# Attention and feed-forward block in float16 pairs on one core: start, weight norms and the order of four steps are rearranged

## The reference

```
x: 4096 tokens (4 sequences of 1024) x 512
x = x + layernorm(attn(layernorm(x)))     # qkv = x @ w_qkv.T + b; 16 heads of 32;
                                          # chunks of 128 tokens, decaying state carried between chunks
                                          # out = attn @ w_out.T + b_out
x = x + layernorm(ffn(layernorm(x)))      # gate, up: 512 -> 1536, down: 1536 -> 512
                                          # weights of ffn rounded to float8 e4m3, scaled by column
gate = silu((x @ e4m3(gate_w)) * gate_scale);  up = (x @ e4m3(up_w)) * up_scale
y = ((gate * up) @ e4m3(down_w)) * down_scale
```

## Time and profile before

| what | us |
|---|---|
| median of 3 runs (1008.97 to 1009.78) | 1009.73 |
| the profiled execution, its own time | 1009.62 |
| its span | 1007.8 |
| TensorE busy | 950.2 (94%) |
| VectorE busy | 666.4 (66%) |
| ScalarE busy | 526.3 (52%) |
| GpSimd busy | 685.0 (68%) |

### The profile page before, as it was taken

How to read it: one execution, slowest core, us unless ns; L and a number is a source line. 1 busy time by engine, 2 the same in 40 slices (tenths; PEclk the granted TensorE clock), 3 DMA queues, 4 the chain that set the end, 5 groups by cost and what they waited for, 6 DMA issues and landing times.

```text
span 1007.8 us, 21799 instructions
## 1 busy us (share of the span) xinstructions
PE 950.2 (94%) x8396; PEld 703.3 (70%) x8396; DVE 666.4 (66%) x1342; ACT 526.3 (52%) x997; POOL 685.0 (68%) x837
## 2 busy tenths in 40 slices
PE   1999997999887999999999999999999999999996
PEld 1777775767665778677786767878677786776764
DVE  7977776765787766676776657766666676766422
ACT  3656565476553646354564545546354564544522
POOL 2788988787756768576685857758567685756633
PEclk9999998999999999999999999999999999999999
DMA  9699799999939957749396693947759386621110
GB/s 345 188 247 257 194 258 251 305 229 253 270 93 217 207 126 154 132 117 196 65 175 119 134 162 90 189 97 146 135 125 190 77 167 118 124 63 43 33 33 21
DMA packets 297640, 159.86 MB, mean 159 GB/s; under 512 B 141632, under 2 KB 272832, under 8 KB 297408
## 3 DMA queue, kind: packets, MB, share of 16 engines
q1 hardware_dynamic: 296672, 157.86, 69.9%
q10 hardware_dynamic: 864, 0.61, 0.2%
HBM read 82.93 MB, written 41.94 MB: 124 GB/s over the span
## 4 chain that ended last, share of the span: by engine, by line
PE 49%; POOL 26%; DVE 12%; issue 5%; ACT 3%; DMA 3%; SPq 1%; POOLq 0%; DVEq 0%; ACTq 0%
PE bank L858 17%; PE bank L844 14%; PE att L821 8%; POOL att_pool L998 6%; POOL w_pool L1012 4%; POOL hl L1008 3%; POOL rstd L939 3%; PE bank L737 3%; PE bank L752 3%; POOL xr L1004 2%; DVE stats L1243 2%; DMA dram_qk<-qk_hl 2%; POOL rstd L943 2%; POOL vv L982 2%; PE att L737 2%
## 5 line engine op out<-in xcount | busy, mean ns | idle before, releaser
L844 PE MATMUL bank<-f_pool,gate_q 128*128 128x256 f16 x1536 | 184.8, 274 | 5.3 <-DMA f_pool<-hl 4.3
L844 PE MATMUL bank<-f_pool,up_q 128*128 128x256 f16 x1536 | 183.7, 273 | 0.0
L858 PE MATMUL bank<-down_q,w_pool 128*128 128x512 f16 x768 | 168.3, 379 | 8.1 <-POOL w_pool L1012 8.1
L998 POOL TENSOR_TENSOR att_pool<-p,att_pool 128x512 f16<-128x512 f32 x128 | 145.6, 1158 | 37.6 <-ACT att_pool L527 37.6
L1374 DVE SCALAR_TENSOR_TENSOR w_pool<-bank,us_t,w_pool 128x256 f32<-128x256 f32 x192 | 84.1, 479 | 126.1 <-PE bank L844 100.7
L844 PEld LDWEIGHTS bank<-f_pool,gate_q 128*128 128x128 f16 x1536 | 147.8, 98 | 25.9 <-DMA f_pool<-hl 4.5
L844 PEld LDWEIGHTS bank<-f_pool,up_q 128*128 128x128 f16 x1536 | 150.6, 98 | 17.6
L936 POOL TENSOR_TENSOR rstd<-mv,eps_t 128x1 f32<-128x1 f32 (+1 forms) x112 | 28.9, 258 | 172.6 <-DVE mv L1246 172.6
L858 PEld LDWEIGHTS bank<-down_q,w_pool 128*128 128x128 f16 x768 | 74.1, 98 | 96.4 <-issue 9.5
L1012 POOL TENSOR_TENSOR w_pool<-w_pool 128x512 f16<-128x512 f32 x96 | 111.0, 1158 | 42.4 <-ACT w_pool L579 42.4
L527 ACT CAST att_pool<-p 128x512 f16<-128x512 f32 x128 | 76.7, 619 | 65.8 <-DVE p L1284 65.8
(11 more groups left out here) (141 smaller groups left out, 1789.2 us busy)
## 6 DMA issues: line engine op xcount, KB each, us to landing
xr<-in_x SPq DMA_DIRECT2D x32, 512.0 KB, 4.6
dram_qk<-qk_hl SPq DMA_DIRECT2D x64, 256.0 KB, 5.4
att_pool<-dram_qk SPq DMA_DIRECT2D x64, 256.0 KB, 6.4
f_pool<-dram_qk SPq DMA_DIRECT2D x64, 256.0 KB, 6.4
dram_v<-vv SPq DMA_DIRECT2D x32, 256.0 KB, 3.8
dram_kd<-kd_hl SPq DMA_DIRECT2D x32, 256.0 KB, 3.3
qn_pool<-dram_qk SPq DMA_DIRECT2D x32, 256.0 KB, 7.8
out_x<-w_pool SPq DMA_DIRECT2D x32, 256.0 KB, 2.1
```

What stands on the lines that cost most here:

```text
L844: ins = nc.tensor.matmul(b[:, j * TOK:(j + 1) * TOK], w[:, k, o * P:(o + 1) * P], x1_hl[:, v % 2, part, k], start=(k == 0 and part == 0), ...
L858: ins = nc.tensor.matmul((b_gate, b_up)[t][:, :], h_hl[:, part, k, t * P:(t + 1) * P], down_q[:, k], start=(k == 0 and part == 0), stop=(k ...
L998: nc.gpsimd.tensor_tensor(pr_hl[:, 1, heads(g)], by_head(p32[:, g % 2]), pr_hl[:, 0, heads(g)], ALU.subtract).then_inc(p_lo_d, 1)
```

## The change

The weights are loaded by columns (q, k, v) and each third gets its own scale; x of unit 0 comes in two halves; v's weights are issued behind turn_x(0); down_s moves from ScalarE's queue to SP's. third() is now all four row tiles by 256 columns. TensorE runs 48 products of constants before the first spread and 16 behind it. The squares and their sums are gone: VectorE takes the row maximum of each rounded piece (row_limit), squares and sums twelve numbers a partition (row_sums), and one product sums them over the partitions (sum_rows, in ahead(12)); scale_h moves behind the lead. kd_hi(k) and kd_lo(k) move into ahead(k). In early(1) the steps of x1 move forward on VectorE, ScalarE and GpSimd. down runs in four parts: products 0 to 9 of both token tiles, then 10 and 11 of both, with later waits.

```diff
         def third(w, part, half):
-            return w[:, 2 * half:2 * half + 2, part * D:(part + 1) * D]
+            return w[:, :, part * D + half * TOK:part * D + (half + 1) * TOK]
...
-            load_x(0)
-            for k in range(KT):
-                sp.dma_start(w_stage[:, k], w_qkv_t[k * P:(k + 1) * P, :]).then_inc(w_in[k], 16)
+            for t in range(T):
+                sp.dma_start(xr[:, 0, t], x_u[0][:, t]).then_inc(x0_in[t], 16)
+            for part in range(3):
+                if part == 2:
+                    turn_x(0)
+                sp.dma_start(w_stage[:, :, part * D:(part + 1) * D],
+                             w_qkv_t.rearrange("(k p) n -> p k n", p=P)[:, :, part * D:(part + 1) * D]
+                             ).then_inc(w_in[part], 16)
             load_x(1)
-            turn_x(0)
@@ ScalarE @@
+            w_hi(0)
+            w_hi(1)
             x_normalise(1)
             x_hi(1)
+            w_hi(2)
 
             def ahead(k):
                 if k:
                     v_hi(k - 1)
                 q_hi(k, 0)
-                if k:
-                    kd_hi(k - 1)
                 q_hi(k, 1)
-                if 2 <= k < 14:
-                    square(k - 2)
                 k_hi(k, 2)
...
                     x_hi(k + 2)
+                kd_hi(k)
@@ TensorE @@
+            def sum_rows():
+                pe.wait_ge(eps_d, 3)
+                pe.wait_ge(row_sum_d, 1)
+                nc.tensor.matmul(b_gate[:, 0:4], ones, row_sum[:, :], start=True, stop=True).then_inc(row_sum_mm, 1)
...
             def ahead(k):
                 if k == 2:
                     spread_wout_max()
                 project_qk(k, 0)
+                if k == 0:
+                    spread_w_max(1)
                 project_qk(k, 1)
+                if k == 0:
+                    spread_w_max(2)
                 project_qk(k, 2)
                 project_qk(k, 3)
-                for n in SUMMED.get(k, ()):
-                    sum_squares(n)
+                if k == 12:
+                    sum_rows()
...
-                down(v, 0)
-                down(v, 1)
+                if projects:
+                    for first, last in ((0, IT - 2), (IT - 2, IT)):
+                        for t in range(T):
+                            down(v, t, first, last)
+                else:
+                    for t in range(T):
+                        down(v, t, 0, IT)
...
+            pe.wait_ge(eps_d, 3)
+            for n in range(48):
+                nc.tensor.matmul(b_up[:, 0:2 * P], warm[:, 0:P], warm, start=True, stop=True)
+            spread_w_max(0)
+            for n in range(16):
+                nc.tensor.matmul(b_up[:, 0:2 * P], warm[:, 0:P], warm, start=True, stop=True)
...
-            def down(v, t):
-                if t == 0:
-                    pe.wait_ge(silu_d, 6 * v + 6)
-                    pe.wait_ge(h_lo_d, 6 * v + 5)
-                for k in range(IT):
-                    if t == 0 and k == IT - 2:
+            def down(v, t, first, last):
+                for k in range(first, last):
+                    if t == 0 and k == 0:
+                        pe.wait_ge(silu_d, 6 * v + 6)
+                        pe.wait_ge(h_lo_d, 6 * v + 4)
+                    elif t == 0 and k == IT - 4:
+                        pe.wait_ge(h_lo_d, 6 * v + 5)
+                    elif t == 0 and k == IT - 2:
                         pe.wait_ge(h_hi_d, 6 * v + 6)
                         pe.wait_ge(h_lo_d, 6 * v + 6)
+                    elif t and k == 0:
+                        pe.wait_ge(h_d, 6 * v + 6)
@@ GpSimd, ahead(k) @@
-                if k:
-                    kd_lo(k - 1)
                 q_lo(k, 1)
                 if k + 2 < units:
                     x_lo(k + 2)
+                kd_lo(k)
@@ VectorE, prepare_qkv @@
+                w_limit(0, 0)
+                w_limit(0, 1)
+                w_scale(0)
+                scale_bias(0)
+                w_limit(1, 0)
+                w_lo(0, 0)
+                w_lo(0, 1)
+                w_limit(1, 1)
+                w_limit(2, 0)
+                w_scale(1)
+                w_limit(2, 1)
+                scale_bias(1)
+                w_lo(1, 0)
+                x_moments(1, 0)
+                w_lo(1, 1)
+                x_moments(1, 1)
+                w_scale(2)
+                scale_bias(2)
+                w_lo(2, 0)
+                w_lo(2, 1)
...
+            def row_limit(n):
+                dve.wait_ge(f_q_d, n + 1)
+                ins = nc.vector.tensor_reduce(row_max[:, n:n + 1], piece_out(n), AX.X, ALU.max,
+                                              apply_absolute_value=True)
+                ins.then_inc(row_max_d, 1)
@@ VectorE, ahead(k) @@
                 k_lo(k, 3)
+                if k < 12:
+                    row_limit(k)
                 if k == 12:
-                    scale_h()
+                    norms()
...
-            norms(2)
-            flag_down()
+            scale_h()
```

More of the change, by code:

```diff
@@ L131, in sandwich @@
         b_y = [att[:, 0:D], att[:, D:2 * D]]
-        w_in = [sem(f"w_in{k}") for k in range(KT)]
+        w_in = [sem(f"w_in{part}") for part in range(3)]
+        x0_in = [sem(f"x0_in{t}") for t in range(T)]
         eye_in = sem("eye_in")
@@ L461, in _, with w_hi @@
         def _(act):
-            def w_hi(dst, src):
-                nc.scalar.activation(dst, src, ACT.Copy, scale=small[:, 11:12]).then_inc(w_hi_d, 1)
-            def square(n):
-                act.wait_ge(f_q_d, n + 1)
-                at_least(act, square_mm, n - 1)
-                nc.scalar.activation(squares(n), piece_out(n), ACT.Square, scale=SQUARE).then_inc(square_d, 1)
+            def w_hi(part):
+                act.wait_ge(w_scale_d, part + 1)
+                for half in range(2):
+                    nc.scalar.activation(third(wqkv_hi, part, half), third(w_stage, part, half), ACT.Copy,
+                                         scale=small[:, 60 + part:61 + part]).then_inc(w_hi_d, 1)
             def normalised(ln, dst, src, t):
@@ L586, in _ @@
             act.dma_start(us_t[:, :], up_s).then_inc(scl_in, 16)
-            act.dma_start(ds_t[:, :], down_s).then_inc(scl_in, 16)
-            x_normalise(0)
-            x_hi(0)
-            act.wait_ge(w_scale_d, 1)
-            for part in range(3):
-                for half in range(2):
-                    w_hi(third(wqkv_hi, part, half), third(w_stage, part, half))
+            for t in range(T):
+                act.wait_ge(rs_d[LN_X], t + 1)
+                normalised(LN_X, x_src(0)[:, t], x_src(0)[:, t], t).then_inc(nrm_d[LN_X], 1)
+                act.wait_ge(nrm_d[LN_X], t + 1)
+                nc.scalar.copy(x_half(0)[:, t, 0], x_src(0)[:, t]).then_inc(x_hi_d, 1)
+            w_hi(0)
+            w_hi(1)
             x_normalise(1)
             x_hi(1)
+            w_hi(2)
             def ahead(k):
@@ L1173, in w_lo @@
+            def w_lo(part, half):
+                dve.wait_ge(w_hi_d, 2 * part + half + 1)
+                nc.vector.scalar_tensor_tensor(out=third(wqkv_lo, part, half), in0=third(w_stage, part, half),
+                                               scalar=col(60 + part), in1=third(wqkv_hi, part, half), op0=ALU.mult,
                                                op1=ALU.subtract).then_inc(w_lo_d, 1)
```

183 lines of the change are left out of this document (91 added, 92 removed).

## The result

The changed kernel takes 1001.0 us (median of 5 runs, 998.17 to 1003.27) where the kernel before took 1009.73: a ratio of 0.9914, 95% interval 0.9893 to 0.9935. Measured again beside the first experiments it took 1002.28 (1000.12 to 1004.48, 6 runs; ratio 0.9924, 0.9909 to 0.9938). It is faster by some 8 us. The forecast of 993.4 promised 16.3; 1001.0 lies in its range, but the gain is little more than half of the forecast's, and it came by another road than any case in the forecast. The profiled execution took 999.63 with a span of 997.8.

The account below looks back on a forecast made before the run. Bound taken as TensorE, so only its idle time or products removed could count. Terms 3.4 - 15.6 + 0.4 - 2.7 - 1.8 = -16.3 took 1009.7 to 993.4 us; range 983 to 1005.

Parts of the forecast that it names:

- rival B: Start keeps its lead (-4) and slots get no new wait (-7 instead of -1.8): 982 to 987 us; chance 0.18.
- the start, +3.4: Start up to unit 2: first projection sooner, but v(0) and unit 2 later, unit 2 at 59.9 instead of 56.46: +3.4 us.
- the lead, -15.6: Units 2 to 13: sums of squares, TensorE's waits for squares and slow products go, 204.9 to 189.3 us: -15.6.
- rival C: Units 7 to 13 bound by transfers, gain shrinks by 8 to 1001 us, with a worse start 1007; chance 0.19.
- the opened ring: In the units, VectorE-GpSimd-VectorE cycle of 16.7 us through kd_lo of the unit before, claimed to open as kd_lo moves.
- rival D: Units 2 to 11: ring lengthened by the reduction to 18.4 us a unit, total 1020 us, slower than before; chance 0.08.
- step 3: First two units with attention: scale_h and ds_t ahead of masked(0,0,0) +0.4 us; x1 sooner in early(1) -2.7 us.
- x1 sooner, -2.7: Early(1): x1's transposes go out at 320.3 instead of 322.9, gate_up(0,0) starts near 324.6 instead of 327.32: -2.7 us.
- the slots, -1.8: Slots, down in four parts: 8.1 us of waits at down go, a new wait for product(v+1,0) costs 6.3: -1.8 us.

Follow-up runs that it names:

- v's weights first: Changed kernel with w_hi(2) put ahead of x_normalise(1) and x_hi(1) on ScalarE: 999.02 us, ratio 0.9892.
- kd's spill sooner: Changed kernel with SP spilling kd(k) right after the turn of unit k+2, ahead of the loads, instead of one unit later: 993.66 us, ratio 0.9856.
- x1 late: Changed kernel with x1's steps of early(1) put back behind the second attention pass on VectorE, ScalarE and GpSimd: 1001.95 us, ratio 0.9925.
- the second trace: Profiled run of the changed kernel, unchanged, measured again beside the first group of experiments: 1002.28 us, ratio 0.9924.
- kd back in all units: Changed kernel with kd's casts of unit k-1 put back inside unit k on ScalarE and GpSimd, in all units: 1027.16 us, ratio 1.0179.
- kd of unit 13 late: Changed kernel with only kd_hi(13) and kd_lo(13) put back into early(0), behind the first probabilities: 998.29 us, ratio 0.9886.
- the nine traces of the table: Traces of the changed kernel twice and seven variants that don't touch this stretch, in which the cast of kd(13) waits for the spill; no single time.

## Why the prediction was right and wrong

Its direction and its range came true, and so did the mechanisms of the start, the lead and the slots. The total did not come by the sum: early(0), which it had at +0.4, took 5.7 more, and this is nearly all that the gain fell short. Two small sums in the text are off and decide nothing. Ten times 0.4 and three times 0.85 are 6.6, not 6.3. And rival B takes 4 for the step from -1.8 to -7, which is 5.2, so its lower end is 981 and not 982; the stated range, from 983, doesn't reach it either way.

**Right in sum, by some luck: the start, +3.4.** It measured +3.04, with v(0) at 35.64 (forecast 35.9), unit 1 at 43.17 (41.1 to 42.4) and unit 2 at 59.50 (59.9). Two errors cancelled. The first projection came at 15.6 rather than 17.4, because the bias landed earlier, and of no use, since v(0) waits for ScalarE; and limits' large reduction ended at 57.4, so that the spread at 58.83 did not wait for it as forecast, while the v products behind the pause lost 2.35 us (7.69 instead of 5.34) instead of 1. That an earlier v(0) is worth something, and that ScalarE's order sets it, is shown by v's weights first.

**Right: the lead, -15.6.** It measured -16.86. The row maximum takes 1.736 us on f16 data, forecast 1.75 from the f32 reduction of this width (1.748): 16-bit data gain nothing. That agrees with the Trainium skill, "VectorE: DVE Perf Modes", "The perf-mode tier table", by which a reduction has only the 1x form. The 1 us for transfers and the 0.4 for spreads weren't needed, and rival C (transfers bound) did not come about on TensorE: the share rose to 1.11 and units kept 15.66. The reason given, the opened ring, is shown by putting it back: 18.35 us a unit for the 18.4 of rival D. The reduction also slows GpSimd by nothing, as the prediction had it: at 63.05 to 64.79 it runs beside kd_lo, which takes its usual 2.27.

**Wrong: step 3, "+0.4" for early(0).** The step priced scale_h and ds_t (2.4 and 1.15); they took 2.0 together and kept nothing waiting long. What it left out is that kd_hi(13), moved into unit 13, has a wait of its own, for the spill of kd(12), and that v_hi, probs_hi and q_hi of early(0) are queued behind it on ScalarE and state_decay behind kd_lo(13) on GpSimd. The text even wrote "kd_lo(13) is gone from GpSimd there" as a gain. The earlier trace rows could not show the wait, since kd_hi stood so late before that its buffer was always free. But ScalarE's waits held its like: the casts of v waited 10.6 us for spills of v, the last time ahead of v(13). From there the wait could be found by asking of the moved instruction what must have ended before it, and following SP's queue, where the spill stood behind loads of unit 1 and the spill of v(12). Measured: +6.1, of which kd's spill sooner takes away all but 0.45.

The closest rival, C, spoke of spills that grow late in the units but put its price on TensorE's projection, not on what follows the lead. Its number, 1001, matches the median by accident.

**Mis-sized: x1 sooner, -2.7.** The gate came some 2 us sooner, and the next wait, for silu, took nearly all of it back. Over early(1) and the head together the term measured -1.2 in the first trace and +0.5 in the second, and the totals with x1 late and sooner (1001.95; 1001.0 and 1002.28) show no difference. The step had stopped at the gate.

**Right in mechanism, with two sizes that cancel: the slots, -1.8.** It measured -1.08. The old wait, forecast and listed at 8.1, was worth 10.4. The new one, forecast at 6.3 and listed at 5.9 in 13 waits, cost 8.2, and the parts' order 1.1 on top of it, 9.3 together. Both terms came out larger than forecast, by 2.3 and 3.0, so the sum came out nearly right. The forecast saw the new wait but kept to the sum of the change as it stood.

## What to carry to other kernels

When a step is moved earlier, look up what it overwrites, who still reads that, and where the reader's transfer stands in its queue: a wait that never showed becomes a link in the chain, and its price falls where the slack of the stage ends, here at the first instruction after the lead. A wait that a profile lists off the critical path (65 us on ScalarE) deserves a look at the stage's last turn. And where a change has a cure for a wait in two layers (later waits, and parts), measure each alone: one of them may hold the whole gain and the other give it back.

## What the runs showed of the hardware

- A listed pause of TensorE costs more than itself. In the slots 0.35 us listed cost 0.51 from row to row, and taking away 8.1 listed made the slots 10.4 shorter. Behind a pause of 4.48 us, 24 products took 5.30 us instead of 2.78, half the pace for nearly all of them (4.48 us in the second trace, behind 5.34); behind one of 5.91 us, 24 wider ones took 7.69 instead of 5.34, half the pace for somewhat under half of them.
- The same pause of 2.33 us ahead of the same 24 products was followed by 2.78 us in one run and by 4.1 to 4.5 in four. The first products' pace could not be told from the pause alone.
- The transfer of v's bias, 256 KB, let VectorE start on the biases at 5.61 us or before in one trace (kd back in all units) and at 9.87 in another (kd of unit 13 late).
- A spill of two times 256 KB at the end of the lead let its buffer go 6.7 us after it was issued, where the median of this transfer from issue to landing is 3.6 us over the whole kernel. In the nine traces of the table the cast behind it started 4.1 to 9.1 us after unit 13's end.
- An absolute maximum over 1536 columns took VectorE 1.736 us in f16 and 1.748 in f32.
